# Attention stages whose maximum and final scores are two strip visits per sequence, four strips wide, with masked keys

## The reference

```
x = x + L0_attn(norm(x))    # 16 heads of 16, rotary q and k, biases    stage a0
x = x + L0_xattn(norm(x), ctx)   # one head of 256, tanh(We [q,k])        stage b0
x = x + L0_ffn(norm(x))     # routed experts, top 1                    stage c0
x = x + L1_attn(norm(x))    # 16 heads of 16, no bias                  stage a1
x = x + L1_xattn(norm(x), ctx, mask)  # 16 heads, masked               stage a2
x = x + L1_ffn(norm(x))     # ternary weights, gelu, norm              stage d1
```

## Time and profile before

| | us |
|---|---|
| median of three runs | 1377.79 |
| the profiled execution | 1381.43 |
| its span, first to last instruction | 1379.3 |
| TensorE busy | 1320.8 (96%) |
| TensorE weight loads busy | 1194.0 (87%) |
| VectorE busy | 985.2 (71%) |
| ScalarE busy | 732.3 (53%) |
| GpSimd busy | 455.4 (33%) |

### The profile page before, as it was taken

The page is one execution under the profiler, slowest core; times in us unless marked ns, Lnnn a source line. Parts: engine busy times, 40 slices in busy tenths (PEclk is TensorE's granted clock), DMA queues, the critical chain, the costliest instruction groups (busy, mean ns, idle before and its releaser), DMA issues. The chain is left out here.

```text
span 1379.3 us, 41633 instructions
## 1 busy us (share of the span) xinstructions
PE 1320.8 (96%) x15764; PEld 1194.0 (87%) x15764; DVE 985.2 (71%) x2431; ACT 732.3 (53%) x1469; POOL 455.4 (33%) x550
## 2 busy tenths in 40 slices
PE   6999999999989999998999999989999999899997
PEld 5889999789979999998889988878888887689987
DVE  6888888656665455563777778667777778668885
ACT  3555555455654454552655566535555556356562
POOL 2212211123222121120000000046556655478884
PEclk9999999999999999999999999999999999899999
DMA  6000000031110000001000000020000000000000
GB/s 235 3 2 0 0 0 2 2 121 38 31 32 1 1 0 0 1 1 55 2 2 0 0 0 1 2 79 17 17 15 15 15 15 2 8 17 31 23 32 31
DMA packets 16772, 29.34 MB, mean 21 GB/s; under 512 B 3648, under 2 KB 7744, under 8 KB 16288
## 3 DMA queue, kind: packets, MB, share of 16 engines
q1 hardware_dynamic: 16672, 27.97, 6.2%
HBM read 23.77 MB, written 4.19 MB: 20 GB/s over the span
## 5 line engine op out<-in xcount | busy, mean ns | idle before, releaser
L891 DVE TENSOR_REDUCE a_row_max<-a_S 128x4 bf16<-128x512 f32 (+1 forms) x384 | 246.9, 683 | 50.6 <-PE a_S L1061 25.8
L784 ACT ACTIVATE a_probs<-a_S 128x512 f32<-128x512 f32 x384 | 209.0, 595 | 115.0 <-PE a_S L1074 59.4
L175 POOL TENSOR_TENSOR all_var_eps<-all_moments,all_ln_eps 128x2 f32<-128x2 f32 x96 | 25.0, 261 | 602.9 <-DVE all_moments L170 602.9
L1029 PE MATMUL a_S<-a_qm_hi,all_odd_split 32*128 32x256 f32 x1536 | 186.9, 301 | 7.2 <-DVE a_row_max L891 4.8
L746 POOL TENSOR_TENSOR a_shifts<-a_add_mask,a_row_max 128x512 bf16<-128x512 bf16 x128 | 134.9, 1070 | 116.3 <-DVE a_row_max L891 116.3
L1029 PEld LDWEIGHTS a_S<-a_qm_hi,all_odd_split 32*128 32x128 f32 x1536 | 131.2, 183 | 41.5 <-issue 25.3
L1020 PE MATMUL a_S<-all_odd_split,a_qm_hi 32*128 32x128 f32 x1536 | 126.8, 283 | 1.7 <-DVE all_odd_weights L1006 1.7
L1029 PE MATMUL a_S<-a_qm_lo,all_odd_split 32*128 32x256 f32 x768 | 108.1, 275 | 0.0
L1087 PE MATMUL a_AV<-a_probs,a_v_pad 128*32 128x128 f32 x3072 | 103.8, 276 | 0.0
L1020 PEld LDWEIGHTS a_S<-all_odd_split,a_qm_hi 32*128 32x128 f32 x1536 | 99.8, 185 | 2.7 <-DVE all_odd_weights L1006 2.5
L789 ACT ACTIVATE a_av_raw<-a_AV 128x512 f32<-128x512 f32 x96 | 57.6, 600 | 76.5 <-PE a_AV L1087 75.4
(11 more groups left out here) (263 smaller groups left out, 3833.7 us busy)
## 6 DMA issues: line engine op xcount, KB each, us to landing
all_cx<-in_ctx_turned SPq DMA_DIRECT2D x16, 256.0 KB, 2.7
all_cx<-in_ctx SPq DMA_DIRECT2D x16, 256.0 KB, 2.7
out_x<-all_x_res SPq DMA_DIRECT2D x16, 256.0 KB, 2.0
all_x_res<-in_x SPq DMA_DIRECT2D x7, 512.0 KB, 7.0
b_routed_wi<-in_L_ffn_wi_W SPq DMA_DIRECT2D x1, 1024.0 KB, 5.1
b_routed_wo<-in_L_ffn_wo_W SPq DMA_DIRECT2D x1, 1024.0 KB, 7.8
all_even_weights<-in_L_ffn_W_fc SPq DMA_DIRECT2D x1, 1024.0 KB, 5.0
all_even_weights<-in_L_ffn_W_proj SPq DMA_DIRECT2D x1, 1024.0 KB, 6.9
```

Of the source, the lines that this page charges most:

```text
L784: act.activation(probs[:, t % STEPS, :], S2[t % 2][:], ACT.Exp, scale=DH ** -0.5).then_inc(exp_ok, 1)
L891: dve.tensor_reduce(row_max[:, t % 4, :], S1[t % 2][:].rearrange("p (h k) -> p h k", h=QH), AXX, ALU.max).then_inc(max_ok, 1)
L1029: pe.matmul(S2[t % 2][:, c * HV * P:(c + 1) * HV * P], k[par][strip, c, tok], q[par][strip, c, b].rearrange("p h t -> p (h t)"), start=(c ...
```

## The change

In the three attention stages:

- The steps of a group are no longer taken in pairs of strips. Per sequence there is one visit for the final scores of all four strips (`scores`, 24 matmuls of 256 columns in six rounds) and one for the maximum scores (`maximum_scores`). A group is `first_half` and `second_half`, one sequence each, and each has: final scores of this sequence, the shifts, maximum scores of the next sequence, weighted values of this one.
- The maximum scores take the plain rounded queries as the weights (`q_hi`) and *masked keys* as the moving side (`km`): two heads in one matmul of 256 columns, so two matmuls per step and not four. `q_hi` and `km` are new; ScalarE makes them (`high_q`, `masked_k`). In a1 the queries are first copied out of PSUM (`plain_q`).
- Banks: five for scores, of which three are shared between the two kinds, one for weighted values (two before), FA and FB. Values now go to FB.
- Queries and keys are projected two groups ahead (the schedule starts at G = -2), values one ahead, output one behind. In a1 VectorE takes the values out (`take_v`).
- In a0 the normalisation of x from the third group on is ScalarE's (`act_normalise`), with an offset by GpSimd (`pool_offset`). These exist already and are used in d1.
- The normalised and transposed x has a second buffer in a0 and a1.
- The next stages' preparations move to other slots; the fold for b0 is cut in three.

TensorE's new order and the new score code:

```diff
+            def s1_pass(b, j, c):
+
+                strip, tok = slice(32 * j, 32 * j + 32), slice(b * P, (b + 1) * P)
+                return pe.matmul(S1[j][:, c * HV * P:(c + 1) * HV * P], q_hi[strip, c, tok],
+                                 km[strip, c, b].rearrange("p h t -> p (h t)"), start=(not cross or c == 0), stop=not cross,
+                                 skip_group_check=True)
...
+            def maximum_scores(G, b):
+
+                if b == 0:
+                    pe.wait_ge(qhi_ok, G + 1)
+                    pe.wait_ge(km_ok, HV * (G + 1))
+                at_least(pe, exp_ok, step(G, b, -1))
+                at_least(pe, max_ok, step(G, b, 0))
+                for c in range(KC):
+                    for j in range(NQ):
+                        last = s1_pass(b, j, c)
...
+            def scores(G, b, par):
+
+                if b == 0:
+                    pe.wait_ge(qmhi_ok, HV * (G + 1))
+                    pe.wait_ge(qmlo_ok, HV * (G + 1))
+                    pe.wait_ge(khi_ok, G + 1)
+                    pe.wait_ge(klo_ok, G + 1)
+                pe.wait_ge(max_ok, step(G, b, NQ - 1))
+                at_least(pe, exp_ok, step(G, b, 0))
                 for i in range(3 * KC):
...
+                    for j in range(NQ):
+                        s2_pass(b, j, par, i // 3, i % 3)
...
+            def first_half(G, parity):
+                odd = 1 - parity
+                if inside(G):
+                    scores(G, 0, parity)
+                if inside(G - 1):
+                    turn((G - 1) * PAIR + 1)
...
+                if inside(G):
+                    shift_scores(G, 0)
+                if not cross and normed_here(G + 2):
+                    transposes(G + 2)
...
+                if inside(G + 1):
+                    values(G + 1, odd)
+                if inside(G):
+                    maximum_scores(G, 1)
+                if inside(G - 1):
+                    turn_back((G - 1) * PAIR + 1)
+                piece(G, 2)
+                if inside(G + 2):
+                    queries(G + 2, parity)
...
+                    weighted_values(G, 0, parity)
...
+            def second_half(G, parity):
+                if inside(G):
+                    scores(G, 1, parity)
+                    turn(G * PAIR)
...
+                if inside(G):
+                    shift_scores(G, 1)
+                piece(G, 5)
+                if inside(G - 1):
+                    output(G - 1)
+                if inside(G + 1):
+                    maximum_scores(G + 1, 0)
+                if inside(G):
+                    turn_back(G * PAIR)
...
+                if inside(G + 2):
+                    keys(G + 2, parity)
+                if inside(G):
+                    weighted_values(G, 1, parity)
```

VectorE's and ScalarE's first halves (second halves left out):

```diff
+            def maxima(G, b, B, seq):
+
+                if inside(G):
+                    max_step(G, b, 0)
+                if not isinstance(B, int) or 0 <= B < NG * PAIR:
+                    out_low(B, seq)
+                if inside(G):
+                    max_step(G, b, 1)
+                    max_step(G, b, 2)
+
+            def first_half(G, parity):
+                odd = 1 - parity
+                if inside(G):
+                    max_step(G, 0, NQ - 1)
...
+                if inside(G + 1):
+                    if rope:
+                        scaled_key(G + 1)
+                    else:
+                        low_k(G + 1, odd)
+                if inside(G + 3) and not at_first(G, -2):
+                    moments_of(G + 3)
...
+                    normalise((G - 1) * PAIR + 1)
...
+                    low_q(G + 1, odd, 0)
+                    if not rope:
+                        low_q(G + 1, odd, 1)
+                if normed_here(G + 2):
+                    norm.dve_low(dve, G + 2, FA, xT_hi[parity], xT_lo[parity])
...
+                maxima(G, 1, (G - 1) * PAIR + 1, 1)
```

```diff
+            def first_half(G, parity):
+                odd = 1 - parity
+                if inside(G - 1):
+                    raw_heads((G - 1) * PAIR + 1)
+                piece(G, 0)
+                if inside(G + 1):
+                    if rope:
+                        masked_q(G + 1, odd, 1)
+                    else:
+                        high_k(G + 1, odd)
+                for j in range(NQ):
+                    if inside(G):
+                        exp_step(G, 0, j)
+                    if j == 1 and normed_here(G + 2):
+                        norm.act_high(act, G + 2, FA, xT_hi[parity])
...
+                    out_high((G - 1) * PAIR + 1, G - 1, 1)
...
+                    high_q(G + 1)
...
+                    masked_k(G + 1, odd, 0)
+                    if not rope:
+                        masked_k(G + 1, odd, 1)
```

More of the change, by code:

```diff
@@ L557, in pe_slot @@
     def pe_slot(self, pe, slot, banks, free):
-        if slot == len(self.pieces) + 1:
-            pe.wait_ge(*free[0])
+        if slot == STEPS + 1:
+            for sem, count in free:
+                pe.wait_ge(sem, count)
             self.add_up(pe, banks[0])
@@ new lines, in half @@
+            def half(G, b, parity):
+                if cross and inside(G):
+                    shift_step(G, b, NQ - 1)
+                if vo_bias and b == 0 and inside(G):
+                    add_bias(G)
+                if b == 0 and inside(G + 3) and not at_first(G, -2):
+                    norm.pool_rstd(pool, G + 3)
+                    if x_dram is not None:
+                        norm.pool_offset(pool, G + 3)
+                for n in range(1 + next_two):
+                    if b == 0 and of_next(G + 3, n):
+                        next_norm.pool_rstd(pool, n)
+                if rope and b == 1 and inside(G + 1):
+                    low_k(G + 1, 1 - parity)
+                if cross and inside(G + b):
+                    for j in range(NQ - 1):
+                        shift_step(G + b, 1 - b, j)
@@ L773, in _ @@
+            def group(G, parity):
+                if at_first(G, -2):
+                    if x_dram is not None:
+                        norm.pool_rstd(pool, 0)
+                    norm.pool_rstd(pool, 1)
+                for b in range(PAIR):
+                    half(G, b, parity)
             schedule(pool, group)
@@ L857, in _, with group @@
+            def group(G, parity):
+                if cross and at_first(G, -2):
+                    act.wait_ge(setup_pe, 1)
+                    for b in range(PAIR):
+                        last = act.activation(q_mul[:, b * P:(b + 1) * P], AV[:, 0:P], ACT.Copy)
+                    last.then_inc(setup, 1)
+                first_half(G, parity)
+                second_half(G, parity)
             schedule(act, group)
@@ new lines, in group @@
+            def group(G, parity):
+                if at_first(G, -2):
+                    if x_dram is not None:
+                        moments_of(0)
+                        norm.dve_normalise(dve, 0)
+                        wt.fold(dve, consts["turn_sign"][:])
+                    else:
+                        if cross:
+                            masks()
+                        moments_of(1)
+                        norm.dve_normalise(dve, 1)
+                first_half(G, parity)
+                if vo_bias and at_first(G, -1):
+                    dve.wait_ge(vo_full, 1)
+                    for b in range(PAIR):
+                        dve.tensor_tensor(row_o[:, b, :], row_o[:, b, :], AV[:, 0:D], ALU.add).then_inc(vo_added, 1)
+                second_half(G, parity)
@@ L1091, in turn @@
-            def turn(B, b):
+            def maximum_scores(G, b):
[7 more added lines that the diff above has]
+                        last = s1_pass(b, j, c)
+                        if c == KC - 1 and not cross:
+                            last.then_inc(s1_full, 1)
+                if cross:
+                    for j in range(NQ):
+                        pe.matmul(S1[j][:], ident_b[:], add_mask[:].rearrange("p h k -> p (h k)"), start=False, stop=True,
+                                  skip_group_check=True).then_inc(s1_full, 1)
@@ new lines, in shift_scores @@
+            def shift_scores(G, b):
+                for j in range(NQ):
+                    pe.wait_ge(shift_ok if cross else max_ok, step(G, b, j) + 1)
+                    for h in range(QH):
+                        part = S2[j][:, h * P:(h + 1) * P]
+                        if cross:
+                            last = pe.matmul(part, shifts[:, j, h, :], ident_b[:], start=False, stop=h == QH - 1,
+                                             skip_group_check=True)
+                        else:
+                            last = pe.matmul(part, row_max[:, j, h:h + 1].to_broadcast([P, P]), neg_ident_b[:],
+                                             start=False, stop=h == QH - 1, skip_group_check=True)
+                    last.then_inc(s2_full, 1)
```

666 lines of the change are left out of this document (310 added, 356 removed).

## The result

The changed kernel takes 1400.2 us (median), the kernel before 1377.8: ratio 1.0158 (from all runs of both), 95% interval 1.0144 to 1.0173. It is slower; the forecast was 1351 us, with a chance of 0.83 for faster. The profiled execution's span is 1398.0 us against 1379.3. The stages that the change doesn't edit took 367.7 and 173.0 us for 368.5 and 174.7; the three attention stages went from 277.3, 255.7 and 303.1 us to 283.6, 264.2 and 309.5.

The account below looks back on a forecast made before the run. TensorE, 96% busy, was taken to bound the loops. The three attention stages were to save 16.1, 3.3 and 6.9 us, together 26.3, giving 1351 us for a median of 1377.8; range 1328 to 1380 for 8 in 10.

Parts of the forecast that it names:

- The strip visits: TensorE in the attention stages: a scores visit costs 0.90 us, a maximum visit 0.43, saving 0.98 us per group.
- Rival 2: Four strips do not overlap fully: rounds of 0.157 us, TensorE saves 0.4 per group, 1367 us in all; chance 0.20.
- Rival 1: No waits at all, TensorE stays the bound in every group: periods 14.3, 14.36 and 16.55 us, 1331 in all; chance 0.12.
- The steady groups: Middle groups of the three attention stages: periods of 14.5, 15.25 and 16.9 us, for 15.28, 15.34 and 17.77 before.
- The heads: From stage start to first scores: 30.0, 12.4 and 23.1 us in the first, second and third attention stage.
- the work ahead comes back at the end, where groups 14 and 15 lack it: Last groups: with queries and keys already done, 11.5 and 10.8 us in the first stage, 12.0 and 9.6 in the second.
- rival 3: Slower hand-over: TensorE waits at every scores visit for VectorE's three maxima and low output; 1409 us in all; chance 0.16.
- Costed at nothing: the later slots of the weight splits: Moving the preparation of the next stages' weights to later slots was given no time in the sum.
- The single bank for the weighted values: Its next use wants the low output, ready 0.3 us before in second halves; uncovered by 0.5, it costs that per half.
- ScalarE's normalisation: First stage, with GpSimd's two small offset operations: costed at nothing; if uncovered, 1.4 us per group.
- wrong altogether: Two signs against the forecast: first scores much after 30 us, or the third stage's last group longer than 22 us.

Follow-up runs that it names:

- e5_high: Changed kernel with the first stage's high keys copied on ScalarE before the high output; ratio 1.0116 to the kernel before.
- e4_head: Changed kernel with the moments of groups 2 and 3 waiting only for the third load of x; ratio 1.0131 to the kernel before.
- e11_three: Changed kernel with the edits of e2_split, e4_head and e5_high together; 1387.3 us, ratio 1.0054 to the kernel before.
- f1_dose: e11_three with one more, unused row maximum in halves 28 to 31 of the first and second stage; ratio 1.0101 to the kernel before.
- e2_split: Changed kernel with the following stage's weight splits moved earlier, to group 13, except b0's folded pieces; ratio 1.0148 to the kernel before.
- e1_bank: Changed kernel with a second bank for the weighted values of the last halves; ratio 1.0153 to the kernel before.
- e6_vnorm: Changed kernel with the first stage's normalisation moved back from ScalarE and GpSimd to VectorE; ratio 1.0141 to the kernel before.
- e8_strip: Changed kernel with scores issued strip by strip in halves 28 to 31 of each stage; ratio 1.0575 to the kernel before.
- e3_fill: Changed kernel with eight unused multiplications before the weighted values of halves 29 to 31, second and third stage; ratio 1.0174 to the kernel before.

## Why the prediction was wrong

*The strip visits.* Right: 0.91 and 0.44 us for 0.90 and 0.43. Rival 2 was false. Here page and measurement differ: by the Trainium skill ("TensorE: Matmul & The Clock Gate", Part 3, Measured speedup) four strips gain 3.07 times, which gave a round of 0.14 us; the six rounds fitted in 0.91, at 0.12 each with the drain. The page's figure is for four tiles of 512 columns, these rounds are of 256. Rival 1, no waits at all, was false as well: from 30 to 245 us TensorE stood idle 8.1 us.

*The steady groups.* Nearly right for the second stage (15.30 for 15.25), and 0.3 and 0.5 us too low for the third and first. The second stage's figure is in part luck. TensorE does wait at the queries for the low transpose, as said, but not the 0.85 us that I had. Two groups in a row:

```profile
789.74 0.50 PE L104 MATMUL a_FA<-all_xT_hi,all_even_split 128*128 128x256 f32 x2 [0.56 <-DVE all_xT_lo L217]
...
805.10 0.50 PE L104 MATMUL a_FA<-a_xT_hi_odd,all_even_split 128*128 128x256 f32 x2 [0.32 <-DVE a_xT_lo_odd L217]
```

Over 13 groups it is 0.44 on average, so TensorE's own work is 14.9 us a group where the sum had 14.36: the change saved it some 0.5 us a group there, not 0.98. Two errors of nearly one size cancelled. In the first stage, 0.35 of the 0.5 is the low key on GpSimd, which I had ending at the moment of its use: e5_high removed it, and the period came to 14.62. The rest I put to the turn: directly behind a strip visit it takes 0.50 us (101.77 to 102.27) where I had 0.36 for it behind shifts, twice a group, 0.3 us together; that was only read, not tested. The third stage's 0.3 wasn't followed up; the trace shows next to no wait of TensorE in its steady groups, so there too it is TensorE's own work that was put too low.

*The heads.* 12.1 and 23.3 us for 12.4 and 23.1. In the first stage 34.5 for 30.0: I hadn't put the landing of x into VectorE's list. e4_head took the wait away, and the first scores came at 29.6. The group after the head was 0.7 to 2.4 us longer than forecast in each stage.

*The step that failed: "the work ahead comes back at the end, where groups 14 and 15 lack it"*, with groups of 9.6 to 12.0 us in the first and second stage. Less work on TensorE makes a shorter group only where TensorE's work is what the half waits for. I used that rule down to 5 us a half and never asked for the longest cycle that is left. The change creates one. Before, scores and maxima had two banks each, and a maximum of one strip lay beside the scores of another. After, both share three of the banks: maximum visit, three maxima, scores visit, shifts, exponentials, maximum visit, one after the other, some 7.07 us a half however little else there is (e11_three; f1_dose for VectorE's part). A steady half of 7.5 us hides it; in the last groups it is the bound, where the kernel before runs at 4 to 6.5 us (second stage). I had seen this row of operations, as rival 3, and put it into the steady groups only, where it took nearly nothing.

*"Costed at nothing: the later slots of the weight splits".* They cost 2.4 to 3.3 us in each of two stages (e2_split, by its trace), as they stand ahead of the maxima in that cycle; moved, they cost half of that in group 13. The single bank for the weighted values, which I gave 0.3 of margin, did wait by 0.93 us in the last groups, and its removal gained nothing (e1_bank): the scores behind it were waiting for maxima. ScalarE's normalisation cost nothing, as said (e6_vnorm).

*The clock.* I had put all rows at 2.4 GHz. In the last groups it fell in most executions (0.83 in 880 to 900 us), and a late half took 7.8 to 9.1 us for 7.07. It doesn't explain the 7.07, but it is no small term. From the scores of half 28 to the end of the second stage, e2_split and e11_three run the same instructions, once partly at 1.2 GHz and once at 2.4 GHz throughout:

```profile
875.70:912.90 37.20, 28.50 (x398) 24.06 (x394) 18.39 (x36) 15.96 (x31) 0.00 (x0) 0.86 0.01 2
```

```profile
866.50:899.70 33.20, 24.51 (x398) 20.42 (x394) 18.39 (x36) 15.95 (x31) 0.00 (x0) 1.00 0.01 2
```

So of the 10.9 us that this stretch missed (39.6 for 28.7) 2.4 are the splits, 4.0 the clock, and 4.5 are left for the cycle and for whatever else the sum had too low. Against the kernel before it lost 8.4 us from turn 26 on, of which 6.3 are gone in e11_three (45.7 to 39.4, for 37.3). In the first stage 37.9 us stand in e11_three for 30.3 forecast, and 44.2 from turn 26 on for 43.3 of before. What is left in e11_three lies mostly in the third stage, which none of its edits touches: 311.3 us for 303.1.

Of the two signs named for "wrong altogether", the first came in a milder form than it was meant (34.5 us), the second by a hair (third stage, 22.4 us from the last group's scores to the end, tail included). The third stage's last groups also hold GpSimd's shifts and VectorE's ternary rounding; which of them sets its halves of 8.2 to 10.2 us was not taken apart.

## What to carry to other kernels

A saving on the bound engine is worth its time only in the stretch where that engine is the bound; for every stretch in which its work thins out (first and last groups), add up the longest cycle through shared buffers, and take the larger. Two uses of one bank that alternate make such a cycle: its length is the sum of all that lies between on every engine, the in-order neighbours of each step included. And a wait that a trace shows is not yet a cost: before removing it, look at what its engine would wait for next.

## What the runs showed of the hardware

Four strips of K=32 with 256 columns each run at the pace of two: 24 matmuls in 0.91 us at 2.4 GHz. One strip's six matmuls alone take 0.88 us (e8_strip, 926.82 to 927.70): the joint visit of four strips costs about what a single strip does. The granted clock behind the same instructions and the same idle time of 2.70 us differed between executions: in the changed kernel the weighted values of half 28 took 1.94 us, in e3_fill 1.08. And the same 398 recorded matmuls at the second stage's end stood in 37.2 us at a mean clock of 0.86 (e2_split) and in 33.2 at 1.00 (e11_three).
